# Causal mask of the diagonal blocks: added in PSUM by VectorE instead of by a TensorE product

## The reference, cut to what matters

```python
attn = jnp.einsum('bhqd,bhkd->bhqk', q, k) / math.sqrt(HEAD_DIM)
attn = attn + alibi_bias(seq_len, N_HEADS)[None] + causal_mask(seq_len)[None, None]
attn = jax.nn.softmax(attn, axis=-1)
y = jnp.einsum('bhqk,bhkd->bhqd', attn, v)
...
x = x + _L0_attn_ref(xn, W_qkv, W_o) + _L0_ffn_ref(xn, wg, W, b)
```

## Time and profile before

| | before |
|---|---|
| median of 3 runs | 1824.9 us (1824.75 to 1836.62) |
| the profiled execution | 1827.11 us, of which the span (first to last instruction) 1825.4 us |
| granted clock of TensorE, mean over the span | 0.97 of full speed |
| busy, share of the span | PE 92%, its weight loads 56%, DVE 61%, ACT 43%, Pool 37% |
| mask products (L1085) | 512 of 128 columns, 118.9 us busy, 232 ns each |

### The profile page before, as it was taken

How to read it: one execution, slowest core, us unless ns; L and a number is a source line. 1 busy time by engine, 2 the same in 40 slices (tenths; PEclk the granted TensorE clock), 3 DMA queues, 4 the chain that set the end, 5 groups by cost and what they waited for, 6 DMA issues and landing times. The chain is left out here.

```text
span 1825.4 us, 27949 instructions
## 1 busy us (share of the span) xinstructions
PE 1687.3 (92%) x9970; PEld 1015.6 (56%) x9971; DVE 1104.7 (61%) x2484; ACT 785.2 (43%) x1575; POOL 675.6 (37%) x643
## 2 busy tenths in 40 slices
PE   5999999579899999999999999999999999689898
PEld 4777777444444444454545444444554443568686
DVE  5333333468677767776876876876777710634466
ACT  2222222024354555564655555565556555411111
POOL 4500000006572552553444454355256256132360
PEclk9999999769999999999999999999999999899899
DMA  6655554744604503602701800900900500355596
GB/s 219 210 185 179 197 189 160 159 77 84 106 8 92 98 13 73 117 7 60 136 7 39 156 8 20 175 8 8 180 16 7 197 7 6 133 161 166 176 393 231
DMA packets 96927, 203.59 MB, mean 112 GB/s; under 512 B 10908, under 2 KB 28348, under 8 KB 91164
## 3 DMA queue, kind: packets, MB, share of 16 engines
q1 hardware_dynamic: 87592, 178.56, 37.8%
q0 software_dynamic: 9216, 23.47, 4.1%
HBM read 122.46 MB, written 79.01 MB: 110 GB/s over the span
## 5 line engine op out<-in xcount | busy, mean ns | idle before, releaser
L1021 ACT ACTIVATE probs_sb<-score_ps 128x512 f32<-128x512 f32 (+3 forms) x1280 | 606.8, 546 | 503.2 <-PE score_ps L1085 196.0
L917 POOL TENSOR_TENSOR pair_sum<-probs_sb 128x512 f32<-128x512 f32 x384 | 480.2, 1283 | 598.7 <-ACT probs_sb L1021 493.1
L940 DVE TENSOR_REDUCE part_max<-max_ps 128x1 f32<-128x512 f32 x768 | 474.2, 680 | 250.4 <-PE max_ps L1050 247.8
L1050 PE MATMUL max_ps<-k_aug,q_aug 104*128 104x512 f32 (+3 forms) x1280 | 534.1, 427 | 54.1 <-DMA q_aug<-q_rows_d 22.8
L1082 PE MATMUL score_ps<-q_aug,k_aug 106*128 106x512 f32 (+3 forms) x1280 | 494.3, 393 | 18.7 <-DMA q_aug<-max_lo 9.8
L1082 PEld LDWEIGHTS score_ps<-q_aug,k_aug 106*128 106x128 f32 x1280 | 243.7, 191 | 183.1 <-issue 112.1
L1050 PEld LDWEIGHTS max_ps<-k_aug,q_aug 104*128 104x128 f32 x1280 | 251.1, 197 | 160.7 <-DVE part_max L940 82.1
L1126 PE MATMUL acc_ps<-probs_sb,v_sb 128*32 128x512 f32 (+3 forms) x2560 | 294.6, 539 | 0.0
L936 DVE CUSTOM_DVE_ANT_0 max_ps<-max_ps,mask_row 128x384 f32<-128x384 f32 (+3 forms) x512 | 238.9, 515 | 57.1 <-PE max_ps L1050 55.6
L972 DVE RECIPROCAL acc_sb<-acc_sb 128x128 f32<-128x128 f32 x128 | 119.7, 940 | 76.6 <-ACT acc_sb L1005 76.6
L1126 PEld LDWEIGHTS acc_ps<-probs_sb,v_sb 128*32 128x32 f32 x2560 | 73.2, 110 | 117.4 <-issue 97.4
(11 more groups left out here) (173 smaller groups left out, 1737.8 us busy)
## 6 DMA issues: line engine op xcount, KB each, us to landing
k_aug<-k_hi_d SPq DMA_DIRECT2D x14, 1024.0 KB
q_aug<-q_hi_d SPq DMA_DIRECT2D x14, 1024.0 KB
slot_y_d<-y_rows SPq DMA_DIRECT2D x39, 256.0 KB, 2.0
xn_d<-xn SPq DMA_DIRECT2D x8, 1024.0 KB, 5.5
q_hi_d<-st_hi SPq DMA_DIRECT2D x32, 256.0 KB, 3.4
q_lo_d<-st_lo SPq DMA_DIRECT2D x32, 256.0 KB, 3.7
k_hi_d<-st_hi SPq DMA_DIRECT2D x32, 256.0 KB, 2.5
k_lo_d<-st_lo SPq DMA_DIRECT2D x32, 256.0 KB, 2.8
```

Of the source, the lines that this page charges most:

```text
L917: nc.gpsimd.tensor_tensor(pair_sum[:, p % 2, hh], probs[:, s0, hh], probs[:, s1, hh], ALU.add).then_inc(pair_added, 1)
L940: nc.vector.tensor_reduce(part_max[:, hh * QT + i, kc:kc + 1], max_ps[:, bank, 0:w], AX.X, ALU.max).then_inc(max_taken, 1)
L1021: nc.scalar.activation(probs[:, r % P_SLOTS, hh, off:CH], score_ps[:, (r * HG + hh) % S_BANKS, off:CH], ACT.Exp).then_inc(exp_done, 1)
L1050: nc.tensor.matmul(max_ps[:, bank, 0:w], q_aug[0:ROW_MAX, half, hh, i * P:(i + 1) * P], k_aug[0:ROW_MAX, half, hh, kc * CH:kc * CH + w], s ...
```

## The change

DVE adds `mask_kq` to the 128 triangle columns of each diagonal score unit, in place in the score bank; PE's mask product is gone, and the score product alone signals `scored`. DVE's addition waits for `scored` and signals a new semaphore `masked`, on which ACT's exp waits in the 16 diagonal rounds (elsewhere it still waits on `scored`). In a diagonal round DVE's order is: addition of head 0, a share of the round's events, addition of head 1, its share, and so on; `shares` cuts the events as PE's order does.

```diff
+MASK_ROUNDS = [r for r, (c, jb) in enumerate(ROUNDS) if jb >= TPC * c]
...
+def shares(events):
+    counted = sum(e[1] in (UNIT, TURN) for e in events)
+    out, seen = [[] for _ in range(HG)], 0
+    for e in events:
+        out[min(hh for hh in range(HG) if seen < counted * (hh + 1) // HG or hh == HG - 1)].append(e)
+        seen += e[1] in (UNIT, TURN)
+    return out
...
+                def add_mask(r, hh, scores):
+                    cc, jb = ROUNDS[r]
+                    off = (jb - TPC * cc) * P
+                    block = score_ps[:, (r * HG + hh) % S_BANKS, off:off + P]
+                    dve.wait_ge(scored, scores + (r * HG + hh + 1))
+                    nc.vector.tensor_tensor(block, block, m.mask_kq[:], ALU.add).then_inc(masked, 1)
...
-                    for r in range(NR):
-                        maxima(events[r], banks, g, units)
+                    scores = base(dve, g, NSU)
+                    for r, (c, jb) in enumerate(ROUNDS):
+                        if jb < TPC * c:
+                            maxima(events[r], banks, g, units)
+                        else:
+                            for hh, share in enumerate(shares(events[r])):
+                                add_mask(r, hh, scores)
+                                maxima(share, banks, g, units)
...
                         for hh in range(HG):
-                            act.wait_ge(scored, units + (r * HG + hh + 1))
+                            if jb >= TPC * cc:
+                                act.wait_ge(masked, rounds_masked + (MASK_ROUNDS.index(r) * HG + hh + 1))
+                            else:
+                                act.wait_ge(scored, units + (r * HG + hh + 1))
...
-                    last = nc.tensor.matmul(score_ps[:, u % S_BANKS, off:CH], k_aug[0:ROWS, half, hh, jb * P:(jb + 1) * P],
-                                            q_aug[0:ROWS, half, hh, cc * CH + off:(cc + 1) * CH], start=True, stop=not diag)
-                    if diag:
-                        last = nc.tensor.matmul(score_ps[:, u % S_BANKS, off:off + P], m.ident_bf[:], m.mask_kq[:],
-                                                start=False, stop=True)
-                    last.then_inc(scored, 1)
+                    nc.tensor.matmul(score_ps[:, u % S_BANKS, off:CH], k_aug[0:ROWS, half, hh, jb * P:(jb + 1) * P],
+                                     q_aug[0:ROWS, half, hh, cc * CH + off:(cc + 1) * CH], start=True, stop=True).then_inc(scored, 1)
```

More of the change, by code:

```diff
@@ L770, in attend @@
             sem("max_blank"), sem("neg_done"), sem("max_turned"), sem("max_hi_done"), sem("max_lo_done"))
+        masked = sem("masked")
         scored, exp_done, pv_done, pair_added, pair_used = (
@@ L1009, in step @@
                     units, rounds, adds = base(act, g, NSU), base(act, g, NR), base(act, g, NPAIR * HG)
+                    rounds_masked = base(act, g, len(MASK_ROUNDS) * HG)
                     for r, (cc, jb) in enumerate(ROUNDS):
@@ L1075, in score_unit @@
                     off = max(0, jb - TPC * cc) * P
-                    diag = jb >= TPC * cc
                     u = r * HG + hh
```

## The result

The changed kernel takes 1925.73 us (median of 4 runs, 1924.48 to 1927.00) against 1825.33 of the kernel before (4 runs): 1.053 times as long, 95% interval 1.050 to 1.056. The forecast was 1876 with a range to 1901. The sign was right, the size was not: 51 us of the 100 were foreseen, and the time lies 25 us above the range. The profiled execution took 1927.0 us, span 1925.3, so 99.9 us more span than before.

The account below looks back on a forecast made before the run. VectorE's chain was taken to bound the diagonal score parts. Longer score parts add 42 us in groups 1 to 6, 5 in group 0, 4 in group 7: 51 on 1827.1 is 1878, from the median 1876; range 1850 to 1901.

Parts of the forecast that it names:

- DVE's chain through unit 4 or 12: Diagonal score parts: length set by when VectorE comes free of unit 4, or unit 12 in the sixteen-unit stretch.
- D was taken for PE's own work: One eight-unit diagonal score part: TensorE alone paced it before (busy 4.27 of 4.27 us); VectorE would pace it after.
- An addition holds DVE for 0.22: Each of 512 mask additions on VectorE: 0.22 us before the next instruction can start, bounds 0.15 to 0.33.
- Score parts 11.21, 6.13, 5.11, 5.21, 5.01, 5.33, 5.51; 6.9 us a group: The seven diagonal score parts of a middle group, in order, in us after the change; together 6.9 us longer.
- PE's saved time shows up nowhere: Diagonal score parts: the 0.96 us TensorE saves per eight units shortens nothing, except through VectorE's earlier start.
- The plain stretches stay: The twelve plain stretches of a group: no spill of VectorE's extra work, so lengths unchanged.
- The value parts stay, 2.71 and 3.15: Value parts behind the diagonal score parts: no spill from VectorE's extra work, so lengths in us unchanged.
- the sum of 42: Groups 1 to 6: 6.9 us a group from longer diagonal score parts, 42 us together.
- 5 forecast: Group 0: 5 us longer, with some additions hidden behind a 3.45 us wait of TensorE for a DMA.
- 4 forecast: Group 7: first three diagonal stretches cost 3.6 us, the other four 0.1 each; 4 us.
- 148.2 was forecast: A middle group of the changed kernel: 148.2 us in all.
- The rival "PE's clock drops": TensorE, standing longer in each score part, falls to its lower clock; 1940 us if throughout the first diagonal stretch; chance 2%.

Follow-up runs that it names:

- The kernel with both masks: Changed kernel with TensorE's mask product put back, so both engines add the mask; 1914.0 us, 1.049 times the kernel before.
- the narrow addition: Changed kernel with TensorE's mask product put back and VectorE adding only 8 of the 128 columns; 1851.8 us, 1.013 times the kernel before.
- the second version: Kernel before without mask product; GpSimd zeroes the triangle after each diagonal exponential, shift of 40 put in VectorE's masked-maxima tile; 1829.6 us, ratio 1.001.

## Why the prediction was right in sign and wrong in size

- *What bounds the diagonal stretches: DVE's chain through unit 4 or 12.* Right. Changing the addition's length alone moved the group by 3.9 us; taking PE's product away moved it by 1.5. One reading in it was off: D was taken for PE's own work, since PE was busy for all of its 4.27 us, but without eight products of 0.12 it still took 4.02. A full busy column did not mean that PE set the length.
- *An addition holds DVE for 0.22.* Right: 0.20 and 0.24.
- *Score parts 11.21, 6.13, 5.11, 5.21, 5.01, 5.33, 5.51; 6.9 us a group.* Right: 11.40, 6.10, 5.01, 5.46, 4.88, 5.31, 5.27, which makes 6.86. A's and D's excess falls in the slow spells; in group 1, where the clock held through D, D is 5.22. G is 0.24 shorter than its sum.
- *PE's saved time shows up nowhere.* Nearly: 1.5 us a group without the additions.
- *The plain stretches stay.* Right, within 0.02.
- *The value parts stay, 2.71 and 3.15.* Wrong, and this is the step that failed: that PE would do its own work behind the longer score parts at the speed of before. The value parts of A, B and D took 5.59, 4.41 and 4.08 us at a clock of 0.55, 0.61 and 0.66. They grew by 5.5 us in group 4, and by more in groups 2 and 5. Of the 80.2 us of groups 1 to 6, some 38 are not in the sum of 42; the same holds for the 9.0 of group 0 (5 forecast) and the 10.7 behind 1508.94 (4 forecast). The kernel with both masks, which has the same chain and in group 4 keeps its clock, takes 148.82 in group 4, where 148.2 was forecast.
- *The rival "PE's clock drops", 2%.* This is what happened beside the forecast's own mechanism. I had priced it (8.3 us a group for all of A, on top of the forecast: 1940) and dismissed it on one row: the clock was 1.00 in B before, where PE waited 0.47 us once. After the change PE waits in most units and once for 1.00 us. The price was of the right order, the place was not (it was paid mostly in the value parts of A, B and D), and the 2% were the error: the clock was taken as a case of its own, but it followed from the forecast's mechanism. In groups 1 to 6 the chain is 41.9 of the 80.2 us and the value parts are 38.3. The trace had a warning. Before, PE was busy for 4.71 of the 5.19 us of B and for 8.30 of 9.26 in A; by my own figures it would be busy for about 0.96 and 1.9 us less in score parts that were 0.94 and 1.95 longer. In B this came out as 4.74 of 6.10 (with products that overlap less), and the clock fell right behind it.

What stays open is why the clock falls in one group or run and not in the next of the same kernel, as with the narrow addition and with both engines adding; no run here was made to tell that. In group 4 of the changed kernel it fell behind B, where PE was busy for 4.74 of 6.10 us, and held behind G, where it was busy for 4.30 of 5.27; in groups 1, 2 and 5 it did not hold there either. Open too is how much of the slow value parts each wait ahead of them is to blame for: the experiments gave PE more work in all diagonal units at once.

## What to carry to other kernels

Work taken off the fullest engine pays only where that engine ends the stretch last; find out which chain ends it, and whether the new work joins that chain. Where a change makes TensorE stand between its products, price the clock as well as the wait, and as a consequence of the wait, not as another case: here it about doubled the loss, and most of it was paid in the next part, whose own code had not been touched. If the work must leave TensorE, look for an engine with time to spare in that very stretch (here Pool): that was level with the kernel before, where the move to VectorE cost 5%. And before work is spread from a crowded stretch to others, look at how much room the crowded engine has there: here VectorE had too little.

## What the runs showed of the hardware

- TensorE's busy time rose by 65 us while it had 512 products less: busy time counts the slow clock. Compare it only together with the clock.
- 1,024 small products added to TensorE beside the chain made the changed kernel 37 us faster: the mean clock went from 0.930 to 0.969, and no more than one value part in a middle group stayed slow.
- One kernel's runs spread from 1841.8 to 1889.3 us with no recorded difference but the mean clock, 0.970 to 0.938, about 15 us for a hundredth. A kernel near this edge should be timed several times, and the clock of each run read beside its time.
- A 128-column VectorE addition in PSUM holds the engine for 0.20 us, one of 8 columns for 0.07. The same in SBUF takes 0.20 alone and up to 0.69 while Pool adds tiles in SBUF.
- GpSimd's cut of a 128x128 triangle in SBUF takes 0.29 us (16 of them 4.63 in stretch A of the second version).
